# Attention loop of a decoder layer: three local reorderings on ScalarE, TensorE and VectorE

## The chip, the cores and the metric

The kernel runs on one core of a Trainium2 chip. The metric is the device time of one launch in microseconds (us). The core's engines each run their own list of instructions in program order and meet only through semaphores: TensorE (PE in the profile; PEld is its weight load), VectorE (DVE), ScalarE (ACT), GpSimd (POOL) and SyncE (SP), which issues DMAs.

## The reference

One decoder layer on x and ctx of shape 8 x 128 x 128 (batch, tokens, features): a bidirectional state-space block, cross-attention with 16 heads of 8 features, and a mixture of 8 experts with top-1 routing; a layer norm follows each. The change touches the attention:

```python
Q = query @ Wq.T
K = key @ Wk.T
V = value @ Wv.T
scores = jnp.einsum('bqhd,bkhd->bhqk', Qh, Kh) / jnp.sqrt(HEAD_DIM)
attn = jax.nn.softmax(scores, axis=-1)
out = jnp.einsum('bhqk,bkhd->bqhd', attn, Vh)
return out.reshape(b, s, N_HEADS * HEAD_DIM) @ Wo.T
...
x = _layernorm(x + _L0_xattn_ref(x, ctx_1024, ctx_1024, Wq, Wk, Wv, Wo))
x = _layernorm(x + _L0_ffn_ref(x, gate_w, w1, w2))
```

## The kernel before

Everything is float32, written as one explicit list of instructions per engine, so the order on an engine is the order of the Python loops. The state-space block fills the first 239 us or so; then come the projections, the attention loop, the routing of tokens to experts (whose tail overlaps the loop's end), the experts and the last norm.

The attention loop works on 16 items: item n is half of the heads (8 of 16) of batch element n // 2, that is scores of 128 queries x 8 heads x 128 keys, 1024 columns wide. Two items make one batch element b. All engines run the same counter i from 0 to 21, each with its own stage of the pipeline:

- PE at i: `scores(i+1)` (two matmuls of 512 columns, L898); at even i from 6 `turn_out(b)` (one transpose); `turn_probs(i-1)`, eight 128x128 transposes of the exps of item i-1 into banks 4 and 5; `weigh_values(i-2)` (L917, 8 heads); at even i from 6 `project_out(b)` (L939). At odd i from 5 there is `turn_values(b)`, four transposes of the weighted values of a batch element, ahead of `turn_probs`. All transposes have the line L681, that of a helper.
- DVE at i: at odd i from 7 the residual of element i // 2 - 3 (L1269, reads the projection `wo`); `shift_scores(i)`, a maximum over 128 keys (L1208) and a subtraction (L1209), each over 1024 columns; at odd i from 5 `normalize_values` (L1215 and L1218, read what `turn_values` wrote); at even i from 8 the moments for the norm (L1178, L1179).
- ACT at i: the exp of item i (L640); the copy of the transposed exps of item i-1 from banks 4 and 5 to SBUF (L649); at odd i the copies of the weighted values and of the turned output (L486).

Dependences around the change: the exp of item n needs the subtraction of n. `turn_probs(n)` needs the exp of n and also that the copy of item n-1 has emptied banks 4 and 5, since there is one pair of these banks (`pT`). The copy of n needs `turn_probs(n)`. `weigh_values(n)` needs the copy of n. `turn_values(b)`, `turn_out(b)` and `project_out(b)` all write bank 7, in turn; so `turn_values(b)` has to wait until the residual of the element before has read bank 7. `normalize_values(b)` needs `turn_values(b)`, and `turn_out(b)` needs `normalize_values(b)`. The scores have two pairs of banks (0 and 1, 2 and 3), the exps three buffers.

The counter ends the score work at item 15. Behind it the last element's values go through the same stages, and the gate of the experts, the routing and the expert matmuls follow, each needing the one before.

Of the kernel before, what the change touches and what calls it, by code (L numbers as in the profile page):

```python
# [22 lines left out]
def decoder_layer_kernel(nc, x, ctx_1024, in_proj_w, conv_w, conv_bias, x_proj_w, dt_proj_w, dt_proj_bias,  # L23
# [42 lines left out]
    with ExitStack() as ctx:  # L66
# [206 lines left out]
        def was_read(name, last):  # L273
            last.then_inc(read[where[name][0]], 1)
# [209 lines left out]
        def _(sc):  # L484
# [150 lines left out]


            for i in range(LAST):
                if i < 2 * B:
                    wait_read(sc, f"s{i}")
                    sc.activation(prob[i % 3], prob[i % 3], ACT.Exp, scale=SCALE).then_inc(exp_ok, 1)  # L640
                if 1 <= i < 2 * B + 1:
                    c = i - 1
                    to_read(sc, f"pT{c}")
                    if c >= 2:
                        if c % 2:
                            to_read(sc, f"av{c // 2 - 1}")
                        else:
                            sc.wait_ge(av_half, c // 2)
                    was_read(f"pT{c}", sc.activation(probT[c % 2].rearrange("p h k -> p (h k)"),  # L649
                                                     bank[:, 4:6, :].rearrange("p a t -> p (a t)"), ACT.Copy))  # L650
                if i % 2 == 1 and 3 <= i < 2 * B + 3:
                    b = i // 2 - 1
                    if b >= 2:
                        to_read(sc, f"avq{b - 2}")
                    evacuate(f"av{b}", avT[b % 2])
                if i % 2 == 1 and 5 <= i < 2 * B + 5:
                    b = i // 2 - 2
                    if b >= 2:
                        to_read(sc, f"wo{b - 2}")
                    evacuate(f"oT{b}", oT[b % 2], lambda ap: ap[:, 0:S])  # L660
                if i == ROUTE0 + 1:
                    route_exp(0)
# [16 lines left out]
        def _(pe):  # L679
# [296 lines left out]
            for i in range(LAST):  # L976
                if 1 <= i < 2 * B - 1:
                    scores(i + 1)
                if i % 2 == 1 and 5 <= i < 2 * B + 5:
                    turn_values(i // 2 - 2)  # L980
                if i % 2 == 0 and 6 <= i < 2 * B + 6:
                    turn_out(i // 2 - 3)
                if 1 <= i < 2 * B + 1:
                    turn_probs(i - 1)
                if 2 <= i < 2 * B + 2:
                    weigh_values(i - 2)
                if i % 2 == 0 and 6 <= i < 2 * B + 6:
                    project_out(i // 2 - 3)
                if i == ROUTE0:
                    gate_logits(0)  # L990
                if i == ROUTE0 + 2:
                    count_tokens(0)
# [35 lines left out]
        def _(ve):  # L1028
# [167 lines left out]
            evacuate("x1T0", x1T[:, half(0)])  # L1196
            normalize(res1, x1, 0, 1, x1_ok)

            def shift_scores(i):

                c = i % 2
# [3 lines left out]
                    to_read(ve, f"pT{i - 3}")  # L1205
                if i >= 2:
                    wait_read(ve, f"s{i - 2}")
                link(ve.tensor_reduce(rmax[:, c, :], src, AX.X, ALU.max))  # L1208
                was_read(f"s{i}", ve.tensor_tensor(prob[i % 3], src, rmax[:, c, :].unsqueeze(2).to_broadcast([P, CH, S]),  # L1209
                                                   ALU.subtract))  # L1210

# [51 lines left out]
                link(ve.tensor_tensor(p_top, p_top, fits, ALU.mult))  # L1263

            for i in range(LAST + 1):
                if i % 2 == 1 and 7 <= i < 2 * B + 7:
                    b = i // 2 - 3
                    src = to_read(ve, f"wo{b}")
                    was_read(f"wo{b}", ve.tensor_tensor(res2[:, b, :], src[:, 0:D], x1[:, b, :], ALU.add))  # L1269
                if i < 2 * B:  # L1270
                    shift_scores(i)
                if i == 3:
                    evacuate("q1", qT[:, half(1)])
                if i % 2 == 1 and 5 <= i < 2 * B + 5:
# [62 lines left out]
```

## Time and profile before

| | us |
|---|---|
| median of 3 runs | 380.46 (380.46 to 384.38) |
| the profiled execution's own time | 382.21 |
| its span | 380.2 |
| PE busy | 298.9 (79% of the span) |
| DVE busy | 288.6 (76%) |
| ACT busy | 247.2 (65%) |
| attention loop, first to last maximum | 247.58 to 295.76 |

Times in rows are us from the start of the span. An engine's row says when an instruction (or a merged group, "x8" being eight of them) starts and how long it takes, then, in brackets, how long its engine was idle just before it and which instruction released it. An instruction on DVE or ACT starts some 0.1 us ahead of the end of the one before where nothing is waited for, so steps are best read from start to start. Ends of PE's instructions are modelled.

### The profile page before, as it was taken

The numbers are of one execution on the slowest core, as the hardware profiler recorded it, in microseconds if no ns is written. First come the engines' busy times: TensorE is split into PE (matmuls) and PEld (weight loads), VectorE is DVE, ScalarE is ACT, GpSimd is POOL, SyncE is SP. The second block draws the span as 40 slices with busy tenths as digits, with TensorE's granted clock in tenths as the row PEclk, the third lists the DMA queues.
The fourth block names the chain that finished last, engine by engine and source line by source line (L and its number), as shares of the span: only waits on it lengthen the run. The fifth ranks groups of instructions, "written<-read, shape, count | busy, mean of one in ns | idle before, by whom it ended". The sixth has DMA issues, their size and how long they took to land.

```text
span 380.2 us, 5350 instructions
## 1 busy us (share of the span) xinstructions
PE 298.9 (79%) x1677; PEld 182.9 (48%) x1677; DVE 288.6 (76%) x456; ACT 247.2 (65%) x448; POOL 197.4 (52%) x131
## 2 busy tenths in 40 slices
PE   4999704999999998999999999889999753089600
PEld 3444404566565644445455457535565542079600
DVE  2757798899999999999999994799788563102335
ACT  2469777899999998999999984757657510022100
POOL 7400644999999998888988850200000105400073
PEclk9999955999999999999999999999999885559955
DMA  6986030322321333322331000000000000210212
GB/s 160 317 244 221 10 108 1 102 96 81 113 100 66 113 110 110 111 85 86 109 111 55 2 1 2 1 0 2 2 2 0 3 0 28 66 32 17 53 42 69
DMA packets 16767, 26.90 MB, mean 71 GB/s; under 512 B 1964, under 2 KB 10308, under 8 KB 16740
## 3 DMA queue, kind: packets, MB, share of 16 engines
q1 hardware_dynamic: 16036, 25.46, 21.3%
q0 software_dynamic: 704, 1.10, 1.0%
q8 instruction: 14, 0.23, 0.2%
q14 instruction: 13, 0.11, 0.1%
HBM read 24.00 MB, written 2.56 MB: 70 GB/s over the span
## 4 chain that ended last, share of the span: by engine, by line
PE 36%; DVE 30%; issue 11%; POOL 10%; ACT 7%; DMA 4%; SPq 0%; POOLq 0%; DVEq 0%; ACTq 0%
DVE arena L1131 19%; PE bank L681 16%; POOL arena L442 6%; PE bank L1008 3%; DVE acc L1141 3%; PE bank L898 3%; PE bank L917 2%; PE bank L1016 2%; PE bank L817 2%; PE bank L741 2%; PE bank L719 2%; POOL arena L478 2%; ACT arena L649 2%; DMA cw<-in_L_attn_convb_w 1%; DMA arena<-dispatched_tokens 1%
## 5 line engine op out<-in xcount | busy, mean ns | idle before, releaser
L442 POOL TENSOR_TENSOR arena<-arena,k_maskT 128x1024 f32<-128x1024 f32 x64 | 150.9, 2382 | 43.0 <-DVE arena L1118 22.4
L1131 DVE TENSOR_TENSOR_SCAN arena<-bank,arena 128x512 f32<-128x512 f32 x128 | 146.0, 1199 | 0.9 <-ACT bank L574 0.9
L681 PE MATMUL bank<-ident,arena 128*128 128x128 f32 (+1 forms) x726 | 110.4, 289 | 43.0 <-DVE arena L1131 23.5
L681 PEld LDWEIGHTS bank<-ident,arena 128*128 128x128 f32 (+1 forms) x726 | 82.1, 145 | 111.3 <-DVE arena L1131 69.8
L574 ACT ACTIVATE bank<-delta,a_neg 128x508 f32<-128x508 f32 x128 | 88.4, 692 | 10.0 <-DVE arena L1131 6.3
L817 PE MATMUL bank<-conv_in_T,ident 128*128 128x512 f32 x192 | 93.7, 598 | 0.0
L585 ACT ACTIVATE conv_in_T<-bank,c_col 128x256 f32<-128x256 f32 x192 | 80.4, 473 | 11.3 <-PE bank L681 10.6
L454 POOL TENSOR_SCALAR rstd<-moments 128x4 f32<-128x4 f32 x6 | 1.4, 242 | 83.4 <-DVE moments L1179 83.3
L817 PEld LDWEIGHTS bank<-conv_in_T,ident 128*128 128x128 f32 x192 | 31.8, 192 | 15.8 <-issue 14.8
L486 ACT ACTIVATE arena<-bank 128x512 f32<-128x512 f32 (+2 forms) x26 | 12.1, 490 | 32.8 <-PE bank L681 27.4
L1038 DVE COPY arena<-bank 128x160 f32<-128x160 f32 (+2 forms) x20 | 8.1, 433 | 30.9 <-PE bank L1016 17.3
L1141 DVE SCALAR_TENSOR_TENSOR acc<-bank,c_col,acc 128x256 f32<-128x256 f32 x64 | 27.4, 468 | 1.5 <-PE bank L681 1.2
L640 ACT ACTIVATE arena<-arena 128x1024 f32<-128x1024 f32 x16 | 16.9, 1057 | 17.6 <-DVE arena L1209 17.6
L478 POOL DMA_INDIRECT arena<-expert_outputs,take_u x8 | 7.6, 954 | 35.1 <-DMA expert_outputs<-arena 32.9
L1208 DVE TENSOR_REDUCE rmax<-bank 128x8 f32<-128x1024 f32 x16 | 19.4, 1215 | 1.8 <-PE bank L898 1.8
L1209 DVE TENSOR_TENSOR arena<-bank,rmax 128x1024 f32<-128x1024 f32 x16 | 19.6, 1224 | 0.5
L898 PE MATMUL bank<-k_maskT,uT 32*128 32x512 f32 x64 | 18.0, 640 | 0.7 <-DVE arena L1209 0.7
L649 ACT ACTIVATE arena<-bank 128x1024 f32<-128x1024 f32 x16 | 16.2, 1010 | 1.9 <-PE bank L681 1.9
L674 ACT ACTIVATE arena<-bank 128x640 f32<-128x640 f32 x8 | 5.6, 704 | 14.1 <-PE bank L1008 14.1
L719 PE MATMUL bank<-xT,conv_in_T 128*128 128x512 f32 x32 | 14.4, 596 | 0.0
L1008 PE MATMUL bank<-arena,w_sb 128*128 128x160 f32 x64 | 12.1, 345 | 0.6 <-DVE arena L1038 0.6
L1008 PEld LDWEIGHTS bank<-arena,w_sb 128*128 128x128 f32 x64 | 11.0, 226 | 1.0 <-issue 1.0
(155 smaller groups left out, 299.1 us busy)
## 6 DMA issues: line engine op xcount, KB each, us to landing
k_maskT<-b_rows SPq DMA_DIRECT2D x32, 512.0 KB, 3.7
w_sb<-in_L_ffn_w SPq DMA_DIRECT2D x1, 2048.0 KB, 10.6
dispatched_tokens<-zeros SPq DMA_DIRECT2D x1, 640.0 KB, 16.4
expert_outputs<-arena SPq DMA_DIRECT2D x4, 160.0 KB, 2.0
x_tok<-in_x SPq DMA_DIRECT2D x1, 512.0 KB, 3.8
ctx_tok<-in_ctx SPq DMA_DIRECT2D x1, 512.0 KB, 4.1
out<-arena SPq DMA_DIRECT2D x2, 256.0 KB, 2.3
arena<-dispatched_tokens SPq DMA_DIRECT2D x1, 384.0 KB, 3.6
```

Of the source, the lines that this page charges most:

```text
L442: gp.tensor_tensor(dBx[g % 2][h], du[:, dr, h, :], b_bc[:, g % RING, :], ALU.mult).then_inc(dBx_ok, 1)
L574: sc.activation(tiles(bank[:, k % DA_BANKS, :], HB)[:, :, inner], tiles(delta[:, dr, h, half(q)], HB)[:, :, inner], ACT.Exp, scale=a_neg[: ...
L585: sc.activation(y_part[:, p, at:at + DI], hT(g, b), ACT.Copy, scale=c_col[:, dr, b, n:n + 1]).then_inc(part_ok, 1)
L649: was_read(f"pT{c}", sc.activation(probT[c % 2].rearrange("p h k -> p (h k)"), bank[:, 4:6, :].rearrange("p a t -> p (a t)"), ACT.Copy))
L681: return pe.transpose(dst, src, ident[0:src.shape[0], 0:src.shape[0]])
L719: last = pe.matmul(dst, wkT[:, dr, k, :], xT[:, group(th), off:off + S], start=(k == 0), stop=(k == K - 1))
L817: last = pe.matmul(bank[:, Y_BANK + p, :], ident[:, :], y_part[:, p, :], start=(g == 0), stop=False, skip_group_check=True)
L898: last = pe.matmul(bank[:, g, :], qT[in_g, S * b:S * b + S], k_maskT[in_g, b, :, :].rearrange("p j k -> p (j k)"), start=True, stop=True)
L1008: last = pe.matmul(bank[:, where[f"h{e}"][0] + c // 2, at:at + CAP], w1_sb[:, e, P * c:P * c + P], xeT[:, CAP * e:CAP * e + CAP], start=Tr ...
L1131: ve.tensor_tensor_scan(o, a, v, 0.0, ALU.mult, ALU.add).then_inc(scanned, 1)
L1141: ve.scalar_tensor_tensor(acc[:, b, :], hT(g, b), c_col[:, dr, b, n:n + 1], acc[:, b, :], ALU.mult, ALU.add).then_inc(acc_ok, 1)
L1209: was_read(f"s{i}", ve.tensor_tensor(prob[i % 3], src, rmax[:, c, :].unsqueeze(2).to_broadcast([P, CH, S]), ALU.subtract))
```

## The change

Three blocks change places; no instruction is added or removed.

1. ACT: in turn i the copy of the transposed exps of item i-1 stands ahead of the exp of item i.
2. PE: at odd i `turn_values` stands behind `turn_probs`.
3. DVE: at odd i from 7 the residual stands between the maximum and the subtraction of item i, where it stood ahead of the maximum. (The last one, at i = 21, and those of i = 17 and 19, where there is no item any more, stand as before.)

```diff
             for i in range(LAST):
-                if i < 2 * B:
-                    wait_read(sc, f"s{i}")
-                    sc.activation(prob[i % 3], prob[i % 3], ACT.Exp, scale=SCALE).then_inc(exp_ok, 1)
                 if 1 <= i < 2 * B + 1:
                     c = i - 1
                     to_read(sc, f"pT{c}")
...
                     was_read(f"pT{c}", sc.activation(probT[c % 2].rearrange("p h k -> p (h k)"),
                                                      bank[:, 4:6, :].rearrange("p a t -> p (a t)"), ACT.Copy))
+                if i < 2 * B:
+                    wait_read(sc, f"s{i}")
+                    sc.activation(prob[i % 3], prob[i % 3], ACT.Exp, scale=SCALE).then_inc(exp_ok, 1)
...
                     scores(i + 1)
-                if i % 2 == 1 and 5 <= i < 2 * B + 5:
-                    turn_values(i // 2 - 2)
                 if i % 2 == 0 and 6 <= i < 2 * B + 6:
                     turn_out(i // 2 - 3)
                 if 1 <= i < 2 * B + 1:
                     turn_probs(i - 1)
+                if i % 2 == 1 and 5 <= i < 2 * B + 5:
+                    turn_values(i // 2 - 2)
...
+            def add_residual(b):
+                src = to_read(ve, f"wo{b}")
+                was_read(f"wo{b}", ve.tensor_tensor(res2[:, b, :], src[:, 0:D], x1[:, b, :], ALU.add))
...
-                link(ve.tensor_reduce(rmax[:, c, :], src, AX.X, ALU.max))
+                steps[0] += 1
+                ve.tensor_reduce(rmax[:, c, :], src, AX.X, ALU.max).then_inc(dve, 1)
+                max_done = steps[0]
+                if i % 2 == 1 and i >= 7:
+                    add_residual(i // 2 - 3)
+                ve.wait_ge(dve, max_done)
...
             for i in range(LAST + 1):
-                if i % 2 == 1 and 7 <= i < 2 * B + 7:
-                    b = i // 2 - 3
-                    src = to_read(ve, f"wo{b}")
-                    was_read(f"wo{b}", ve.tensor_tensor(res2[:, b, :], src[:, 0:D], x1[:, b, :], ALU.add))
                 if i < 2 * B:
                     shift_scores(i)
+                elif i % 2 == 1 and i < 2 * B + 7:
+                    add_residual(i // 2 - 3)
```

The rows below are the instruction lists themselves, with the semaphores that each waits for. On ACT, at the loop's start (exps of items 0, 1 and 2, copies of items 0 and 1), before the change:

```order
L640 ACTIVATE arena<-arena 128x1024 [waits bank0_read]
L640 ACTIVATE arena<-arena 128x1024 [waits bank2_read]
L649 ACTIVATE arena<-bank 128x1024 [waits bank4_full]
L640 ACTIVATE arena<-arena 128x1024 [waits bank0_read]
L649 ACTIVATE arena<-bank 128x1024 [waits bank4_full]
```

And at the same place with the change, where the exp has the line L650 and the copy L646:

```order
L650 ACTIVATE arena<-arena 128x1024 [waits bank0_read]
L646 ACTIVATE arena<-bank 128x1024 [waits bank4_full]
L650 ACTIVATE arena<-arena 128x1024 [waits bank2_read]
L646 ACTIVATE arena<-bank 128x1024 [waits bank4_full]
L650 ACTIVATE arena<-arena 128x1024 [waits bank0_read]
```

The copy of item i-1, which waits for the transposes (`bank4_full`), now stands ahead of the exp of item i, which waits for the subtraction (`bank0_read` or `bank2_read`).

On PE, at an odd turn in the loop's middle: the scores, the transposes of the values (`bank7_read,bank6_read`), those of the exps (`exp_ok`) and the weighing of the item before.

```order
 L898 MATMUL bank<-k_maskT,uT 128x512 [waits bank7_read,bank2_read,bank0_read]
 L898 MATMUL bank<-k_maskT,uT 128x512
-L681 MATMUL bank<-ident,arena 128x128 [waits bank7_read,bank6_read]
-L681 MATMUL bank<-ident,arena 128x128 x3
-L681 MATMUL bank<-ident,arena 128x128 [waits bank4_read,exp_ok]
-L681 MATMUL bank<-ident,arena 128x128 x7
+L681 MATMUL bank<-ident,arena 128x128 [waits bank4_read,exp_ok]
+L681 MATMUL bank<-ident,arena 128x128 x7
+L681 MATMUL bank<-ident,arena 128x128 [waits bank7_read,bank6_read]
+L681 MATMUL bank<-ident,arena 128x128 x3
 L917 MATMUL bank<-arena,delta 32x128 [waits bank4_read,bank1_read]
 L917 MATMUL bank<-arena,delta 32x128 x7
```

The eight transposes of the exps start by the length of four transposes earlier in PE's list, and those of the values eight later.

On DVE, from the moments of an even turn to the normalization of the odd turn behind it, before the change:

```order
L1178 BN_STATS stats<-arena 128x6 [waits bank7_read]
L1179 BN_AGGR moments<-stats 128x2 [waits dve_steps]
L1269 TENSOR_TENSOR arena<-bank,x_tok 128x128 [waits bank7_full]
L1208 TENSOR_REDUCE rmax<-bank 128x8 [waits bank2_read,bank4_full,bank2_full]
L1209 TENSOR_TENSOR arena<-bank,rmax 128x1024 [waits dve_steps]
L1215 RECIPROCAL inv_sum<-bank 128x16 [waits bank7_full]
```

And with it, where the residual is L1201, the maximum L1213, the subtraction L1218 and the reciprocal L1224:

```order
L1178 BN_STATS stats<-arena 128x6 [waits bank7_read]
L1179 BN_AGGR moments<-stats 128x2 [waits dve_steps]
L1213 TENSOR_REDUCE rmax<-bank 128x8 [waits bank2_read,bank4_full,bank2_full]
L1201 TENSOR_TENSOR arena<-bank,x_tok 128x128 [waits bank7_full]
L1218 TENSOR_TENSOR arena<-bank,rmax 128x1024 [waits dve_steps]
L1224 RECIPROCAL inv_sum<-bank 128x16 [waits bank7_full]
```

The wait for the projection (`bank7_full` of the residual) has moved behind the maximum.

## Rows read from the trace of the kernel before

**Rows 1.** Chain of waits in the loop: start us, length us, engine, tile, line
```profile
254.60 1.06 PE bank L681 x8
...
257.30 1.02 PE bank L681 x8
258.32 0.57 PE bank L917 x16
258.89 1.06 PE bank L898 x4
...
265.70 1.13 PE bank L681 x9
...
275.80 1.46 PE bank L681 x12
277.26 0.62 PE bank L917 x16
...
279.61 1.06 PE bank L681 x8
280.68 0.57 PE bank L917 x16
281.25 0.42 PE bank L939 x2
```

**Rows 2.** Timeline of DVE, a late pair of turns and the last residual of interest
```profile
281.70 0.29 DVE L1269 TENSOR_TENSOR arena<-bank,x_tok 128x128 f32<-128x128 f32 x1 [0.95 <-PE bank L939]
281.91 1.22 DVE L1208 TENSOR_REDUCE rmax<-bank 128x8 f32<-128x1024 f32 x1
283.16 1.22 DVE L1209 TENSOR_TENSOR arena<-bank,rmax 128x1024 f32<-128x1024 f32 x1
284.30 0.25 DVE L1215 RECIPROCAL inv_sum<-bank 128x16 f32<-128x16 f32 x1
...
284.79 1.22 DVE L1208 TENSOR_REDUCE rmax<-bank 128x8 f32<-128x1024 f32 x1
...
288.84 1.22 DVE L1208 TENSOR_REDUCE rmax<-bank 128x8 f32<-128x1024 f32 x1
...
303.88 0.29 DVE L1269 TENSOR_TENSOR arena<-bank,x_tok 128x128 f32<-128x128 f32 x1 [3.74 <-PE bank L939]
```

**Rows 3.** Timeline of ACT: the loop's start, a turn that waits, a late pair, the end
```profile
250.10 1.06 ACT L640 ACTIVATE arena<-arena 128x1024 f32<-128x1024 f32 x1 [2.99 <-DVE arena L1209]
252.49 1.06 ACT L640 ACTIVATE arena<-arena 128x1024 f32<-128x1024 f32 x1 [1.33 <-DVE arena L1209]
...
264.11 1.02 ACT L649 ACTIVATE arena<-bank 128x1024 f32<-128x1024 f32 x1 [0.40 <-PE bank L681]
...
277.50 1.06 ACT L640 ACTIVATE arena<-arena 128x1024 f32<-128x1024 f32 x1 [2.07 <-DVE arena L1209]
278.46 1.01 ACT L649 ACTIVATE arena<-bank 128x1024 f32<-128x1024 f32 x1
279.37 0.76 ACT L486 ACTIVATE arena<-bank 128x512 f32<-128x512 f32 x2
...
298.26 1.06 ACT L640 ACTIVATE arena<-arena 128x1024 f32<-128x1024 f32 x1 [2.07 <-DVE arena L1209]
299.23 1.01 ACT L649 ACTIVATE arena<-bank 128x1024 f32<-128x1024 f32 x1
```

**Rows 4.** Timeline of PE: first and fifth items' transposes, the last item's
```profile
251.21 1.09 PE L681 MATMUL bank<-ident,arena 128*128 128x128 f32 x8
...
262.54 1.53 PE L681 MATMUL bank<-ident,arena 128*128 128x128 f32 x12
...
300.38 1.94 PE L681 MATMUL bank<-ident,arena 128*128 128x128 f32 x8 [1.21 <-ACT arena L649]
```

**Rows 5.** Stretches: length, busy us (x) of PE, PEld, DVE, ACT, POOL; granted clock; DMA
```profile
276.00:283.00 7.00, 6.54 (x66) 4.01 (x65) 5.92 (x10) 4.59 (x6) 0.00 (x0) 1.00 0.00 0
...
301.00:302.00 1.00, 1.00 (x7) 0.92 (x5) 0.00 (x0) 0.00 (x0) 0.00 (x0) 0.50 0.07 16
...
306.00:308.00 2.00, 1.12 (x10) 1.03 (x9) 1.07 (x3) 0.24 (x1) 0.00 (x0) 1.00 0.00 0
```

## Prediction

> **What bounds the kernel now.** I read the stretches first, then the chain of waits in the attention loop, then the timelines of PE, ACT and DVE there. The change touches only this loop, from 247.6 us to some 304 us; before and behind it nothing moves but the start time. In the stretch 276 to 283 PE is busy 6.54 of 7 us, DVE 5.92 and ACT 4.59, at granted clock 1.00 [rows 5], which is 2.4 GHz: PE is the nearest to its limit.
>
> I write T(n) for the start of the eight transposes of the exps of item n, and follow T from item to item.
>
> *Early loop.* From T(1) at 254.60 on, the chain of waits is PE work alone. A turn is transposes 1.02, weighing 0.57, scores 1.06 [rows 1], together 2.65 us. ACT does not bind: the exp of the next item is done well ahead of its transposes, because it stands ahead of the copy.
>
> *Late loop.* A pair of turns lasts 288.84 - 281.91 = 6.93 us [rows 2]. PE's own work in it is 1.46 + 0.57 + 1.06 for the odd turn, 0.11 for the one transpose of the output (nine transposes 1.13 against eight 1.02), and 1.02 + 0.57 + 0.42 + 1.06 for the even turn [rows 1]: 6.27. The rest, 0.66, is one stall: the even turn's transposes (279.61) wait for the copy that empties their banks. That copy starts at 278.46, behind the exp, and the exp starts only at 277.50, when the subtraction is done, ACT having been idle for 2.07 us [rows 3]. So the copy, whose data lie ready since about 277.3 (the twelve transposes of 275.80 end 1.46 later, rows 1 say), waits 1.2 us behind an exp that waits for DVE. The chain runs through the copy (1.01) to PE. DVE too waits in each pair, 0.95 us for the projection ahead of the residual [rows 2]; its work is 6.93 - 0.95 = 5.98 us a pair.
>
> **The change part by part.** No instruction comes or goes; what counts is the new cycle.
>
> *Copy ahead of exp (ACT).* In the late loop this takes the stall's cause away. But it makes a cycle that wasn't there: transposes of item n-1, their copy, the exp of item n (now behind that copy), transposes of item n. Its length c, from rows:
> - transposes to the waiting copy: 264.11 less the start of the eight. They stand behind four others in the twelve that start at 262.54 [rows 3, 4], so at 262.54 + (1.46 - 1.02) = 262.98; 1.13 us. Where PE itself had waited the group is 1.06 and not 1.09 long [rows 1, 4]: 1.10.
> - copy to the next instruction on ACT: 279.37 - 278.46 = 0.91 [rows 3].
> - the exp: 1.06 [rows 3].
> - exp's end to the transposes: 251.16 to 251.21, 0.05 [rows 3, 4]. The nearest other row, a copy's end (279.47) to the transposes at 279.61 [rows 1, 3], gives 0.14, the upper bound. PE was just done with its scores at 251.2 too, so 0.05 hides nothing longer.
>
> So c = 1.10 + 0.91 + 1.06 + 0.05 = 3.12, at most 3.21 with 0.14. **The early loop loses:** 3.12 to 3.21 where it had 2.65, with PE idle 0.5 us a turn. In the late loop c and PE are nearly equal.
>
> *T(n) worked out.* T(0) stays at 251.21 [rows 4]. The copy of item 0 starts at 251.21 + 1.13 = 252.34 (before: behind the exp of 252.49); exp of item 1 at 253.25, ends 254.31; T(1) = 254.36 to 254.45 (before 254.60 [rows 1]). Three cycles: T(4) = 263.72 to 264.08, where it was 262.98. This costs 0.7 to 1.1 us. From T(4) a pair is the larger of PE and cycle in each step: even to odd item PE 1.46 + 0.57 + 1.06 + 0.11 = 3.20 against c = 3.12 to 3.21; odd to even item PE 3.07 against c with 1.13 in place of 1.10, so 3.15 to 3.24. A pair is 6.35 to 6.45. Five pairs: T(14) = 295.5 to 296.3. There are no scores left in the step to item 15, so PE is idle and the step is c: T(15) = 298.6 to 299.5. It was 300.38 [rows 4]. **Gain up to T(15): 0.8 to 1.8; I take the middle, 1.3 us**, since each row bounding c is of this very pair of operations or its neighbour.
>
> *Values behind exps (PE).* Costed in the 3.20 above: with the four transposes in front, the even-to-odd cycle would be 0.44 longer (3.56 to 3.65), so this move is what lets the first one pay, 5 times 0.36 or more. Its price is that the values come 1.02 later, and DVE's normalization with them: filled at T(even) + 1.46 + some 0.1, so DVE normalizes from T + 1.55, is through at T + 2.04 (284.30 to 284.79, 0.49 [rows 2]), and does the next maximum and subtraction (1.25 + 1.22 [rows 2]) by T + 4.5. The exp that needs it may start at T + 3.20 + 1.13 + 0.91 = T + 5.2. Cover: 0.7 us. DVE's own pair is 5.98 or less against 6.4, so it doesn't fall behind.
>
> *Residual between maximum and subtraction (DVE).* The wait for the projection, 0.95 us a pair, now lies behind the maximum. Price on DVE: the residual's step was 0.21 (281.70 to 281.91) and the subtraction waits 1.25 behind the maximum anyway, of which about 0.1 is the gap to an instruction that needn't wait (283.16 to 284.30 is 1.14) [rows 2], so it now costs about 0.1, gain 0.1 a pair on an engine that has 0.4 to spare: nothing in the sum. The value transposes wait for this residual (bank 7); it is done about 1.4 behind the maximum's start, near T(even), and they come at T + 1.02: covered by 1 us. Queued behind the residual's wait are the subtraction and so the odd exp. The projection is ready 2.09 behind the odd T (279.61 to 281.70 [rows 1, 2]), the subtraction is over 1.6 later, at about +3.7, and the odd exp has until about 5.2: cover 1.5 us. No DMA and no queue of SP is passed in any of the moves.
>
> *The end.* At T(15) PE has waited 1.21 us, and the group takes 1.94 instead of 1.02; the stretch 301 to 302 has granted clock 0.50, that is 1.2 GHz [rows 4, 5]. From T(15) to the residual it is 303.88 - 300.38 = 3.50 us [rows 2, 4], where the same work at 2.4 GHz takes 2.09 (above). In the changed kernel PE waits here too, about 1.1 ahead of T(14) and some 0.7 to 0.9 around T(15), with 2.0 us of dense work (twelve transposes and weighing) between. The stretch 306 to 308, with PE busy 1.12 of 2 us, kept clock 1.00 [rows 5]. So I think it likelier than not (about two to one, a judgement and not a row) that T(15) still finds 2.4 GHz: **gain 1.4 us more.** Everything behind (residual, values, gate, routing, experts) hangs on this one step after another and moves as a whole.
>
> The Trainium skill ("TensorE: Matmul & The Clock Gate", section "A second HAM failure mode: psum-queue depth-cycling") speaks against this: in a kernel whose TensorE idles briefly and often between groups, the clock swung between its two levels. The early loop gets just such gaps, 0.5 us in each 3.1. By the rows of this case there is no swing at 0.46 us idle in each pair; by that rule rival 4 would happen, at its price.
>
> **Sum.** 1.3 + 1.4 = 2.7 us. The profiled execution took 382.21 with a span of 380.2; the median of the runs is 380.46. The change is a difference inside the loop, so I take it from the median: 380.46 - 2.7 = **377.8 us**, 0.7% less.
>
> **The rivals.**
> 1. *The order works as above, but the clock at T(15) is 1.2 GHz as before.* Gain 0.8 to 1.8: 379.2 us. For it: PE's idle share around T(14) to T(15) is nearly the old one.
> 2. *Slower, by a longer cycle.* If the exp behind the copy doesn't start 0.1 ahead of the copy's end but 0.05 behind it, and exp to PE is 0.14, then c = 1.13 + 1.01 + 0.05 + 1.06 + 0.14 = 3.39 and T(15) = 254.5 + 14 x 3.39 = 302.0: 1.6 later, 382.1 us. It decides from c = (300.38 - 254.4) / 14 = 3.28 on. Against it: every exp and copy that stand back to back in the rows overlap by 0.1.
> 3. *More gain.* PE alone sets the late loop (6.27), c is 3.1 or less, and the chain behind T(15) loses more gaps (the clock also stays up in the routing): 4 us or more, 376.3. Only the clock speaks for it.
> 4. *The clock falls in the loop*, in the early turns with 0.5 us of idle each. The same PE work at half the clock takes nearly double (1.94 for 1.02): each pair so run costs up to 6 us; one or two give 384 to 390 us. Against it: clock 1.00 with 0.46 idle of 7 and, later, with 0.88 idle of 2 [rows 5].
>
> **How the numbers follow.** About 1% (3.8 us) is what a measurement of this kernel can tell from no change. Forecast 0.50 (own range 376.6 to 378.9), rival 1 0.22, rival 2 0.13, rival 3 0.07, rival 4 0.08. The forecast, rival 1 and rival 2 lie within 1% (382.1 is 0.4%). Faster by over 1%: rival 3 and the very edge of the forecast, 0.09. Slower by over 1%: rival 4, 0.08. Within: 0.83. The range from 376.4 to 381.4 holds the forecast, rival 1, half of rival 2 and a little of rival 3.
>
> **What the profile after would show.** ACT in the early loop alternates copy and exp with PE as the releaser of each copy, T(n) 3.1 to 3.2 apart and PE idle 0.5 ahead of each; T(4) near 263.9. The late pair is near 6.4 us with no stall above 0.15 on PE. The residual has a wait behind the maximum but the exps none for DVE. T(15) near 299, eight transposes in 1.02. I am wrong if an exp in the late loop still names DVE's subtraction as its releaser (then the covers above were too thin), if T(n) are over 3.28 apart, or if a stretch inside the loop has a clock below 1.

## The result, and the profile after

| | before | changed |
|---|---|---|
| median of 15 runs each, us | 381.28 (379.63 to 386.54) | 378.01 (376.98 to 380.23) |
| ratio of the runs | | 0.9897, 95% interval 0.9871 to 0.9923 |
| span of the profiled execution | 380.2 | 376.5 |
| PEclk in the stretch 297 to 304 | 0.76 | 1.00 |

The forecast was 377.8 from 380.46, a ratio of 0.993; the measured one is 0.9897. The range 376.4 to 381.4 holds the time. The ratio leaves out the run of 386.54, over 1.5% above the fastest of its kernel, and is not the quotient of the two medians (0.9914).

The two traces don't start the loop at the same time: the first maximum is at 247.58 before and at 246.41 after, 1.17 us that arose ahead of all that the change touches (over the fourteen traces of this document it lies anywhere from 245.34 to 247.58). So from here on I count from the first maximum, and write T(n), as the prediction does, for the start of the eight transposes of item n's exps.

The early turns first. Chain of waits of the changed kernel (start us, length us, engine, tile, line; L646 is the copy, L650 the exp):

```profile
253.19 1.11 PE bank L681 x8
254.31 0.62 ACT arena L646
254.93 0.30 issue
255.24 1.06 ACT arena L650
256.34 1.11 PE bank L681 x8
```

Where [rows 1] had PE work alone, the chain now runs round the predicted cycle: transposes, copy, exp, transposes, from 253.19 to 256.34, so 3.15 us a turn in place of 2.65. ACT's timeline gives its terms:

```profile
251.16 1.02 ACT L646 ACTIVATE arena<-bank 128x1024 f32<-128x1024 f32 x1 [1.18 <-PE bank L681]
252.08 1.05 ACT L650 ACTIVATE arena<-arena 128x1024 f32<-128x1024 f32 x1
...
276.47 1.02 ACT L646 ACTIVATE arena<-bank 128x1024 f32<-128x1024 f32 x1 [1.18 <-PE bank L681]
277.39 1.05 ACT L650 ACTIVATE arena<-arena 128x1024 f32<-128x1024 f32 x1
278.33 0.80 ACT L486 ACTIVATE arena<-bank 128x512 f32<-128x512 f32 x2
279.67 1.02 ACT L646 ACTIVATE arena<-bank 128x1024 f32<-128x1024 f32 x1 [0.54 <-PE bank L681]
```

Copy to exp is 0.92, the exp 1.05. Behind the loop's very first exp none waits for DVE any more, where [rows 3] had 2.07 us of it in each late pair; every copy waits for PE. PE's timeline, with the start, the late pair and the end:

```profile
250.04 1.09 PE L681 MATMUL bank<-ident,arena 128*128 128x128 f32 x8
...
253.19 1.09 PE L681 MATMUL bank<-ident,arena 128*128 128x128 f32 x8 [0.72 <-ACT arena L650]
...
262.64 1.53 PE L681 MATMUL bank<-ident,arena 128*128 128x128 f32 x12 [0.43 <-ACT arena L650]
...
275.34 1.53 PE L681 MATMUL bank<-ident,arena 128*128 128x128 f32 x12
...
278.43 1.20 PE L681 MATMUL bank<-ident,arena 128*128 128x128 f32 x9
...
281.69 1.53 PE L681 MATMUL bank<-ident,arena 128*128 128x128 f32 x12
...
294.39 1.53 PE L681 MATMUL bank<-ident,arena 128*128 128x128 f32 x12 [1.07 <-ACT arena L650]
...
297.55 1.09 PE L681 MATMUL bank<-ident,arena 128*128 128x128 f32 x8 [0.55 <-ACT arena L650]
```

T(0) to the copy is 251.16 - 250.04 = 1.12; the exp's end at 253.13 to T(1) is 0.06. The late pair is 281.69 - 275.34 = 6.35, with no stall left that the timeline reports. T(4) is at 16.23 from the first maximum (15.40 before), T(14) at 47.98 (48.85), T(15) at 51.14 (52.80). At T(15) the group takes 1.09 and not 1.94: the clock is at 2.4 GHz. DVE in the same pair and at the end:

```profile
280.22 1.23 DVE L1213 TENSOR_REDUCE rmax<-bank 128x8 f32<-128x1024 f32 x1
281.36 0.28 DVE L1201 TENSOR_TENSOR arena<-bank,x_tok 128x128 f32<-128x128 f32 x1
281.56 1.22 DVE L1218 TENSOR_TENSOR arena<-bank,rmax 128x1024 f32<-128x1024 f32 x1
283.25 0.26 DVE L1224 RECIPROCAL inv_sum<-bank 128x16 f32<-128x16 f32 x1 [0.48 <-PE bank L681]
...
299.67 0.29 DVE L1201 TENSOR_TENSOR arena<-bank,x_tok 128x128 f32<-128x128 f32 x1 [1.70 <-PE bank L939]
```

The residual of this pair doesn't wait at all now (0.95 before, [rows 2]), the subtraction starts 1.34 behind the maximum instead of 1.25, and DVE's remaining wait is for the value transposes. The residual of element 5 is the loop's last step that everything behind hangs on: 299.67 - 246.41 = 53.26, where it was 303.88 - 247.58 = 56.30. That is 3.04 us, 1.66 up to T(15) and 1.38 for the clock behind it. Behind this residual the changed kernel's trace is 0.51 us longer (76.83 to the end of the span, against 76.32), so the spans differ by 1.17 + 3.04 - 0.51 = 3.70 us; of these the 1.17 lie ahead of all that was changed.

### The profile page after: what moved, and what is told of

Read it like the earlier page. It is cut to its first block, busy times and chain, and to the rows that moved or that the text cites. A ratio compares the mean times of both kernels' runs of the same rounds, so it can differ in the third digit from the quotient of the medians.

```text
span 376.5 us, 5350 instructions
## 1 busy us (share of the span) xinstructions
PE 296.3 (79%) x1677; PEld 182.3 (48%) x1677; DVE 288.3 (77%) x456; ACT 246.6 (66%) x448; POOL 197.3 (52%) x131
## 4 chain that ended last, share of the span: by engine, by line
PE 38%; DVE 29%; POOL 10%; issue 9%; ACT 8%; DMA 4%; SPq 1%; POOLq 0%; DVEq 0%; ACTq 0%
DVE arena L1131 19%; PE bank L681 17%; POOL arena L442 6%; PE bank L817 3%; PE bank L898 3%; PE bank L1008 3%; DVE acc L1141 3%; PE bank L1016 2%; PE bank L741 2%; PE bank L719 2%; POOL arena L478 2%; PE bank L917 2%; ACT arena L650 2%; ACT arena L646 1%; DMA cw<-in_L_attn_convb_w 1%
## 5 line engine op out<-in xcount | busy, mean ns | idle before, releaser
L681 PE MATMUL bank<-ident,arena 128*128 128x128 f32 (+1 forms) x726 | 109.3, 288 | 41.7 <-DVE arena L1131 23.2
L646 ACT ACTIVATE arena<-bank 128x1024 f32<-128x1024 f32 x16 | 16.4, 1023 | 14.6 <-PE bank L681 14.6
L1213 DVE TENSOR_REDUCE rmax<-bank 128x8 f32<-128x1024 f32 x16 | 19.5, 1219 | 1.9 <-PE bank L898 1.8
L1218 DVE TENSOR_TENSOR arena<-bank,rmax 128x1024 f32<-128x1024 f32 x16 | 19.5, 1222 | 0.4
L650 ACT ACTIVATE arena<-arena 128x1024 f32<-128x1024 f32 x16 | 16.8, 1048 | 3.0 <-DVE arena L1218 3.0
```

The costliest lines, as they stand in the source:

```text
L681: return pe.transpose(dst, src, ident[0:src.shape[0], 0:src.shape[0]])
```

## The experiments

One table first. T(15), the residual of element 5, and the late pair (distance of two late residuals) come from each trace, times from the runs. All ratios are to runs of the kernel before in the same comparison; their medians were 381.28 for the changed kernel, 382.91 for e1 to e4 and 383.37 for e5 and e6, so ratios of different comparisons differ by some tenths of a per cent for this reason alone.

| kernel | late pair | T(15) | residual 5 | median us | ratio (95%) |
|---|---|---|---|---|---|
| before | 6.92 | 52.80 | 56.30 | 381.28 | 1 |
| changed (ACT, PE, DVE) | 6.35 | 51.14 | 53.26 | 378.01 | 0.9897 (0.9871 to 0.9923) |
| e1: ACT | 6.66 | 52.34 | 54.46 | 378.69 | 0.9914 (0.9875 to 0.9954) |
| e2: DVE | 6.27 | 48.94 | 51.04 | 375.1 | 0.9821 (0.9728 to 0.9914) |
| e3: PE | 6.92 | 52.80 | 54.89 | 380.27 | 0.9968 (0.992 to 1.0016) |
| e4: PE, DVE | 6.66 | 51.17 | 53.26 | 377.97 | 0.9893 (0.9796 to 0.9989) |
| e5: ACT, PE | 6.35 | 51.15 | 53.28 | 377.78 | 0.9859 (0.9777 to 0.994) |
| e6: ACT, DVE | 6.66 | 52.34 | 54.46 | 378.5 | 0.9895 (0.9815 to 0.9974) |

My theory was that each step lasts as long as the longest of PE's work, ACT's cycle and DVE's, and that the changed kernel's gain comes from the copy's new place. The rival, which I worked out once the trace showed that the residual waits no more, was that the wait of the residual ahead of the maximum had been the cause all along.

### One part at a time

e1, the ScalarE part alone:

```diff
-                if i < 2 * B:
-                    wait_read(sc, f"s{i}")
-                    sc.activation(prob[i % 3], prob[i % 3], ACT.Exp, scale=SCALE).then_inc(exp_ok, 1)
                 if 1 <= i < 2 * B + 1:
...
                                                      bank[:, 4:6, :].rearrange("p a t -> p (a t)"), ACT.Copy))
+                if i < 2 * B:
+                    wait_read(sc, f"s{i}")
+                    sc.activation(prob[i % 3], prob[i % 3], ACT.Exp, scale=SCALE).then_inc(exp_ok, 1)
```

> Only the ScalarE part of the change (copy ahead of the next exp). Distances are from the start of the first maximum; before / changed kernel: T(4) 15.40 / 16.23, T(15) 52.80 / 51.14, residual of element 5 at 56.30 / 53.26. Theory 'the longest of PE work, ACT cycle and DVE' (ACT cycle now measured as 3.15): early turns 3.15, T(4) 16.2; in the late loop TensorE meets the value transposes ahead of those of the exps, 3.07 + 0.44 = 3.51 in one step, 3.15 in the other, so a pair of 6.66; T(15) near 52.3, residual 5 at 54.4 (full clock) or 55.8 (half clock). Time 0.5 to 1.9 us below before. Rival 'the order on ScalarE by itself does all the work': pair 6.35 and the time of the changed kernel, 3.3 us or more below before.

Measured: pair 6.66, T(15) 52.34, residual 54.46, each within 0.1 us of the theory. The rival falls in the loop. The time did not follow: 378.69 is 4.2 us below the median of 382.91 beside it and not 0.5 to 1.9, because ten of those 19 runs lie in an upper bunch (below) that none of e1's ten shows; below the median of the seven runs in the lower bunch, 380.22, it is 1.5. One late pair of e1, first on ACT, then on PE:

```profile
276.29 1.02 ACT L646 ACTIVATE arena<-bank 128x1024 f32<-128x1024 f32 x1 [1.54 <-PE bank L681]
277.21 1.05 ACT L650 ACTIVATE arena<-arena 128x1024 f32<-128x1024 f32 x1
...
278.31 1.09 PE L681 MATMUL bank<-ident,arena 128*128 128x128 f32 x8 [0.17 <-ACT arena L650]
```

The copy waits only for its transposes, and PE no longer waits for the copy but 0.17 us for the exp behind it. So the copy's new place does take the old stall away, and puts the cycle of 3.15 us in its place.

e2, the VectorE part alone (the kernel before, with the third part of the change's diff):

```diff
-                if i % 2 == 1 and 7 <= i < 2 * B + 7:
-                    b = i // 2 - 3
...
+                if i % 2 == 1 and i >= 7:
+                    add_residual(i // 2 - 3)
...
                 if i < 2 * B:
                     shift_scores(i)
+                elif i % 2 == 1 and i < 2 * B + 7:
+                    add_residual(i // 2 - 3)
```

> Only the VectorE part (residual between maximum and subtraction). Theory 'the wait for the projection sat on the path through subtraction and exp': with it behind the maximum the odd subtraction ends 1.2 us earlier, the exp too, so the copy behind the exp starts when the transposes are done; ScalarE's order needn't change. Then the early turns keep 2.65 (T(4) 15.4), a late pair is TensorE's own 6.27, T(15) near 49.0, residual 5 near 51.1 at full clock: 5 us below before, 2 us below the changed kernel. Rival, from the prediction's account of the stall (the copy's place behind the exp is its cause): the stall stays, pair 6.9, no change within 0.5 us; or a small part of it.

Measured: pair 6.27, T(15) 48.94, residual 51.04. PE's timeline of a late pair:

```profile
272.84 1.53 PE L681 MATMUL bank<-ident,arena 128*128 128x128 f32 x12
...
275.93 1.20 PE L681 MATMUL bank<-ident,arena 128*128 128x128 f32 x9
...
279.11 1.53 PE L681 MATMUL bank<-ident,arena 128*128 128x128 f32 x12
```

No group in this pair, of those left out here either, has idle time ahead of it: the nine transposes of 275.93 (one of the output, eight of exps) run on, where the kernel before had this wait for the copy:

```profile
279.61 1.06 PE L681 MATMUL bank<-ident,arena 128*128 128x128 f32 x8 [0.46 <-ACT arena L649]
```

So with the exp still ahead of the copy, the stall is gone as well. It had two conditions, a copy that stood behind an exp and an exp that waited for a late subtraction, and taking away either is enough: e1 and e5 remove the first, e2 the second. The prediction saw only the first. The early turns keep 2.65 us, since nothing joins copy and exp into a cycle.

e3, the TensorE part alone:

```diff
-                if i % 2 == 1 and 5 <= i < 2 * B + 5:
-                    turn_values(i // 2 - 2)
...
                 if 1 <= i < 2 * B + 1:
                     turn_probs(i - 1)
+                if i % 2 == 1 and 5 <= i < 2 * B + 5:
+                    turn_values(i // 2 - 2)
```

> Only the TensorE part (value transposes behind those of the exps). Theory 'the subtraction sets the odd exp': the even transposes come 0.44 earlier and nobody uses it; pair 6.93, residual 5 at 56.3, no change within 0.4 us. Rival 'every part carries a share': a third of the gain, some 1 us below before.

Measured: pair 6.92 and T(15) 52.80, both unchanged, as the theory had it. The residual of element 5 came at 54.89, 1.41 earlier than expected, since the last eight transposes took 1.07 here, at 2.4 GHz, though the wait ahead of them was the same 1.21 us:

```profile
297.85 0.30 PE L681 MATMUL bank<-ident,arena 128*128 128x128 f32 x1 [0.45 <-DVE arena L1218]
299.37 1.07 PE L681 MATMUL bank<-ident,arena 128*128 128x128 f32 x8 [1.21 <-ACT arena L649]
```

That is a matter of the clock, taken up below.

### Two parts at a time

The edits are the three diffs above in pairs: e4 has those of e2 and e3 (the change without the swap on ScalarE), e5 those of e1 and e3 (without the move on VectorE), e6 those of e1 and e2 (without the move on TensorE).

> The change without its ScalarE part. Theory as for the VectorE part alone: early turns 2.65, pair 6.27, T(15) near 49.3, residual 5 near 51.4 at full clock: about 5 us below before, 1.9 below the changed kernel, the same as the VectorE part alone within 0.4 us. Rival 'the copy must stand ahead of the exp': not better than the changed kernel, pair above 6.35.

Measured: pair 6.66 and not 6.27, residual 53.26 and not 51.4: 2.2 us worse than the VectorE part alone. The expectation failed, and the trace shows why. Timeline of e4 over one pair, all engines (L1218 is the subtraction, L1224 and L1227 the normalization of the values):

```profile
274.30 1.50 PE L681 MATMUL bank<-ident,arena 128*128 128x128 f32 x12 [0.34 <-ACT arena L649]
...
275.83 0.26 DVE L1224 RECIPROCAL inv_sum<-bank 128x16 f32<-128x16 f32 x1 [0.79 <-PE bank L681]
...
276.33 1.21 DVE L1213 TENSOR_REDUCE rmax<-bank 128x8 f32<-128x1024 f32 x1
...
277.58 1.23 DVE L1218 TENSOR_TENSOR arena<-bank,rmax 128x1024 f32<-128x1024 f32 x1
...
278.84 1.06 ACT L640 ACTIVATE arena<-arena 128x1024 f32<-128x1024 f32 x1 [0.78 <-DVE arena L1218]
...
279.80 1.00 ACT L649 ACTIVATE arena<-bank 128x1024 f32<-128x1024 f32 x1
...
280.95 1.50 PE L681 MATMUL bank<-ident,arena 128*128 128x128 f32 x12 [0.34 <-ACT arena L649]
```

Read from top to bottom it is a closed circle: the values, now behind the exps' transposes, are ready 1.53 after T (275.83); the normalization takes 0.50, maximum and subtraction to 278.81; the exp, then the copy behind it (279.80), then the next transposes at 280.95. That is 6.65 us, longer than PE's 6.27. My expectation had counted one pair and not followed the circle into the next. So the TensorE part is worth something only together with the ScalarE part; it costs 2.2 us (53.26 less 51.04) on top of the VectorE part, and nothing alone (e3).

> The change without its VectorE part: copy ahead of exp, values behind exps, residual ahead of the maximum as before. Theory 'once the copy stands ahead of the exp, the ACT cycle (3.15) and TensorE's work (3.17) set the steps, and VectorE has cover': the odd subtraction ends 4.8 behind the odd T two items before, the exp is wanted at 5.2, so nothing is lost; pair 6.35, T(15) 51.1 and residual 5 at 53.3 from the first maximum, as in the changed kernel; time equal to it within 0.4 us. Rival 'the VectorE part carries the gain in the changed kernel as it does alone': pair above 6.6, 1.5 us or more slower than the changed kernel.

Measured: pair 6.35, residual 53.28, against 53.26 of the changed kernel. The residual, ahead of the maximum as before, still waits for the projection, but the exp just ahead of it in time does not wait for DVE (first a row of ACT, then one of DVE):

```profile
281.44 1.05 ACT L650 ACTIVATE arena<-arena 128x1024 f32<-128x1024 f32 x1
281.51 0.29 DVE L1269 TENSOR_TENSOR arena<-bank,x_tok 128x128 f32<-128x128 f32 x1 [0.37 <-PE bank L939]
```

Once the copy stands ahead of the exp, the residual's place is of no matter: the prediction's "nothing in the sum" for it holds.

> The change without its TensorE part: values stay ahead of the exps' transposes. Theory: 3.07 + 0.44 = 3.51 and 3.15, so a pair of 6.66 as with the ScalarE part alone; residual 5 at 54.4 from the first maximum (full clock); 1.2 us slower than the changed kernel. Rival 'with VectorE ahead TensorE's order is of no matter, as with the VectorE part alone': 6.35 or less, residual at 53.3 or earlier.

Measured: pair 6.66, residual 54.46: 1.20 behind the changed kernel, the same as e1. That is what the TensorE part gives where the ScalarE part is in.

e11 takes the ScalarE swap only from turn 5 on, all else as changed:

```diff
+                if i < 5:
+                    wait_read(sc, f"s{i}")
+                    sc.activation(prob[i % 3], prob[i % 3], ACT.Exp, scale=SCALE).then_inc(exp_ok, 1)
                 if 1 <= i < 2 * B + 1:
...
-                if i < 2 * B:
+                if 5 <= i < 2 * B:
```

> The changed kernel, but with the copy ahead of the exp only from turn 5 on; turns 0 to 4 keep the exp first. Theory 'the early loss is the ScalarE cycle and nothing else': T(4) at 15.40 and not 16.23, pair 6.35 from there, residual 5 at 52.4; 0.8 us below the changed kernel. Rival 'the early loss is made good anyway, since TensorE or VectorE bind later': residual at 53.26.

Measured: the copy of item 4 starts at 16.09 and not 17.36, so T(4) is 1.27 us earlier than in the changed kernel (14.96: I had forgotten that the four value transposes no longer stand ahead of it); pair 6.35; residual 51.99, 1.27 less. The early loss is real and is the ScalarE cycle. Its time is 377.25 (376.77 to 378.82, 4 runs), ratio 0.9898 (0.9832 to 0.9964): 0.5 us under the changed kernel beside it (e9 below, 377.74), within what these runs can tell. The traces say where the rest of the 1.27 went: from residual 5 to the end e11 takes 77.69 us and e9 76.71, and the clock falls to 1.2 GHz 57 us behind the first maximum in e11 and 60 us behind it in e9.

### The clock at the end of the loop

The 69 comparison runs of the kernel before lie mostly in two bunches, 379.3 to 380.6 and 382.5 to 386.5, with seven between. Where the clock of each run is known (54 of them, with e1 to e12), the upper bunch has a mean granted clock of 0.891 to 0.894 over the whole span, every other run 0.898 to 0.912. So the bunches go with TensorE's clock. (The profiled execution of the kernel before, 382.21 at 0.904, lies between them.) e7 adds eight transposes to it, read by nobody, in PE's last wait:

```diff
+                if i == 2 * B:
+                    wait_read(pe, "s14")
+                    for h in range(CH):
+                        turn(bank[:, h // 4, S * (h % 4):S * (h % 4) + S], ident[:, :])
                 if 1 <= i < 2 * B + 1:
                     turn_probs(i - 1)
```

> The kernel before with 8 transposes of the unit matrix, whose results nobody reads, put into TensorE's last wait, ahead of the exps' transposes of item 15. Theory 'the clock fell there because TensorE waited': T(15) stays at 52.8 from the first maximum, the group takes 1.02 and not 1.94, residual 5 at 54.9 and not 56.3; time 1.4 us below before. Rival 'the clock there doesn't hang on this wait' (the TensorE part alone also kept 2.4 GHz with the same wait of 1.21): the kernel before itself, run beside it, shows 54.9 too, and there is no difference between the two.

e8 is the kernel before, run beside it.

> The kernel before once more, for its trace: does the fall to 1.2 GHz at T(15) come back? If it belongs to the kernel's own waits: residual 5 at 56.3 again. If it is a matter of where the execution happens to stand: 54.9. The loop itself (T(4) 15.4, pair 6.92, T(15) 52.8) is to repeat within 0.05.

PE's timeline at the end, e7:

```profile
297.96 0.30 PE L681 MATMUL bank<-ident,arena 128*128 128x128 f32 x1 [0.80 <-DVE arena L1222]
298.10 1.04 PE L681 MATMUL bank<-ident 128*128 128x128 f32 x8
299.48 1.06 PE L681 MATMUL bank<-ident,arena 128*128 128x128 f32 x8 [0.34 <-ACT arena L649]
300.47 0.64 PE L917 MATMUL bank<-arena,delta 128*32 128x128 f32 x16
```

and e8:

```profile
299.64 1.06 PE L681 MATMUL bank<-ident,arena 128*128 128x128 f32 x8 [1.21 <-ACT arena L649]
300.63 1.08 PE L917 MATMUL bank<-arena,delta 128*32 128x128 f32 x16
...
302.92 1.09 PE L681 MATMUL bank<-ident,arena 128*128 128x128 f32 x4 [0.47 <-DVE arena L1269]
```

Two stretches of four us, e8 and then e7 (length, busy us of PE, PEld, DVE, ACT, POOL; granted clock; DMA):

```profile
304.00:308.00 4.00, 3.12 (x27) 2.34 (x26) 1.62 (x5) 0.60 (x1) 0.00 (x0) 0.50 0.00 0
...
304.00:308.00 4.00, 2.34 (x15) 2.05 (x16) 2.20 (x10) 0.46 (x2) 0.00 (x0) 0.90 0.00 0
```

T(15) is 52.80 in both, to 0.01. In e8 the fall comes one group later than in the trace of before (the weighing 1.08 instead of 0.64), so neither of my two answers was right as put: the fall came back, at another place, and residual 5 was at 55.65, between 54.89 and 56.30. With the wait filled it did not come there: residual 5 at 54.89, and the granted clock stayed 1.00 up to 307.2. It fell then in e7 too. In fact every one of the fourteen traces has such a fall, at some time from 300.1 to 307.2; what differs is how much work of the chain lies behind it and whether the clock comes back. In the trace of before it was back at 303.5 and cost 1.41 us, all of it ahead of residual 5. In e8 it fell near 300.6 and stayed at 1.2 GHz: 0.76 us up to residual 5, and 2.64 more up to the next residual (7.94 us, against 5.30 in e7). Together with 0.25 behind, that is the 3.65 us by which e8's trace is longer than e7's from the first maximum on.

All ten runs of e7 are from 379.30 to 380.02, with clocks of 0.904 to 0.912, where seven of the ten of e8 are 383.05 and more. The medians are 379.62 and 383.1, the ratios to before 0.9927 (0.9891 to 0.9963) and 0.999 (0.9942 to 1.0039). So filling 1.04 of 1.21 us of one wait, with the loop's schedule untouched, takes away 3.5 us of median. That filling this wait keeps the runs out of the upper bunch is shown. That the wait alone brings on the fall is not: e3's trace has the same wait of 1.21 us without a fall there, and two of e3's ten runs (382.98 and 384.58, clocks 0.894 and 0.892) lie in the upper bunch. What decides in which runs stays open.

This splits the result of the change, roughly. Against the kernel before without the early fall (e7, 379.62) the changed kernel's 378.01 is 1.6 us less, near the 1.66 of T(15); but the two medians are of different comparisons (by the ratios it is 1.1 us), and from the first maximum to the end the changed trace is 1.23 us shorter than e7's: 1.63 at residual 5 and 0.39 behind it won, 0.79 lost behind the experts' first matmul. The rest of the change's gain is that its runs don't show the upper bunch (376.98 to 380.23, clocks 0.906 to 0.911). It shortens PE's idle time ahead of T(15) from 1.21 to 0.55 (297.55 above), but lengthens that ahead of T(14) from 0.48 to 1.07 (294.39 above). That the shorter wait is the reason is argued from e7, not tried on the changed kernel itself.

e12 takes e2 and fills two longer waits behind the loop:

```diff
+            def keep_busy(name, n):
+                dst = to_fill(pe, name)
+                for k in range(n):
+                    turn(dst[:, S * (k % 4):S * (k % 4) + S], ident[:, :])
+
+            keep_busy("x2T1", 12)
             gate_logits(1)
             count_tokens(1)
+            keep_busy("xeT0", 48)
```

> The VectorE part alone plus transposes of the unit matrix, read by nobody, in two waits of TensorE behind the loop: 12 ahead of the second gate (it waits 4.2 us there) and 48 ahead of the tokens' transposes (10.7 us). Theory 'TensorE is at 1.2 GHz behind these waits because it idled': the second gate's two groups take 0.63 and 1.03 (not 1.12 and 1.85), the tokens' transposes and the first expert matmuls 3.7 in all (not 6.65); some 4 us below the VectorE part alone, 371. Rival 'the added transposes end too late, or the clock doesn't rise by them': no gain, or slower by what they overrun.

Measured: 376.1 us (373.9 to 376.94, 4 runs), ratio 0.9839 (0.9773 to 0.9906), no better than the VectorE part alone beside it (e10 below, 375.51 and 0.9841), though one run, 373.9, is below all of that kernel's. In the profiled execution, the longest of the four, the theory failed at both places. PE's timeline of e12:

```profile
307.09 2.77 PE L681 MATMUL bank<-ident 128*128 128x128 f32 x12
311.49 1.12 PE L681 MATMUL bank<-ident,ctx_tok 128*128 128x128 f32 x4 [1.63 <-DVE ctx_tok L1191]
...
316.77 8.26 PE L681 MATMUL bank<-ident 128*128 128x128 f32 x48
327.65 0.66 PE L681 MATMUL bank<-ident,arena 128*128 128x128 f32 x4 [2.62 <-DMA arena<-dispatched_tokens]
328.93 1.13 PE L681 MATMUL bank<-ident,arena 128*128 128x128 f32 x6 [0.62 <-DMA arena<-dispatched_tokens]
330.69 4.60 PE L1015 MATMUL bank<-arena,w_sb 128*128 128x160 f32 x16 [0.63 <-DVE arena L1045]
335.08 1.82 PE L1023 MATMUL bank<-arena,w_sb 128*128 128x160 f32 x8
```

The twelve, 2.77 us at 1.2 GHz, didn't raise the clock (the gate's four transposes still take 1.12). The forty-eight did, near 322.6 us, so the first four of the tokens' transposes took 0.66. But 2.62 us of waiting lay between, and the clock fell again near 329.4, during the six transposes; it was back only near 336, so the experts' first two groups took 4.60 + 1.82. In e2, where the clock was back near 332.7, these took 3.99 and 1.25:

```profile
329.51 3.99 PE L1008 MATMUL bank<-arena,w_sb 128*128 128x160 f32 x16 [0.63 <-DVE arena L1038]
333.34 1.25 PE L1016 MATMUL bank<-arena,w_sb 128*128 128x160 f32 x8
```

What was won at the transposes (0.46 and 0.41, from 1.12 and 1.54 in e2) was lost here (0.61 and 0.57).

### The better version

e9 and e10 are the changed kernel and the VectorE part alone, once more and side by side.

> The changed kernel once more, beside the VectorE part alone and under the same comparison runs: ratio to the kernel before 0.988 to 0.990; residual of element 5 at 53.26 from the first maximum.

> The VectorE part alone once more, next to the changed kernel. Theory (its loop is 2.2 us shorter, 51.04 against 53.26, and nothing behind gives that back): 2 to 3 us less than the changed kernel, 375.3. Rival 'the loop's 2.2 us are lost in the routing, where the clock falls earlier': the two kernels within 1 us.

Measured: e9 377.74 us (377.0 to 379.49, 12 runs), ratio 0.9908 (0.9876 to 0.9939), just above the 0.988 to 0.990 expected, residual 5 at 53.26. e10 375.51 us (374.72 to 375.85, 6 runs), ratio 0.9841 (0.9793 to 0.9888), residual 5 at 51.03. The difference of the medians is 2.2 us, the same as in the loop (53.26 - 51.03), and no run of e10 is as long as the shortest of e9. The third part of the change alone beats all three together. Whether it is more or less than 2% below the kernel before, its interval leaves open.

## Why the prediction was right, and where it was wrong

**The ScalarE cycle.** Forecast 3.12 to 3.21; measured 3.15, made of 1.12, 0.92, 1.05 and 0.06 against 1.10, 0.91, 1.06 and 0.05. Right, and the early loop lost 0.83 us up to T(4) (forecast 0.7 to 1.1).

**The late pair.** Forecast 6.35 to 6.45, measured 6.35. T(14) forecast at 295.5 to 296.3 on the old time axis: measured 47.98 + 247.58 = 295.56. T(15) forecast 298.6 to 299.5, measured 298.72. I took the middle of the range, a gain of 1.3; it was 1.66, since the exp to PE took 0.06 and not 0.14. The value came from the row of this very pair of operations (0.05), and I should have trusted it over the neighbour's.

**The clock.** Forecast 1.4 us at two to one, measured 1.38 between these two traces: T(15) at 2.4 GHz. But as a term of the sum it was misread. I took the clock of one profiled execution as a fixed trait of the kernel before; e3, e7 and e8 show that it falls so early in some executions and not in others, at places that differ, and that this is worth 3.5 us between the medians of e8 and e7. It works on the median by how often it comes, not by 1.4.

**The sum.** 2.7 forecast, 3.04 in the loop of the two traces, 3.3 between the medians, 1.03% by the ratio, right at the edge of what I called the same. That 377.8 met 378.01 is partly luck. The median of three runs from which I subtracted, 380.46, lies in the lower bunch, where all runs of e7 lie too, so there was hardly 1.4 us of clock to win on it; with the 1.66 of T(15) alone it would have given 378.8. The median of 15 runs, 381.28, was 0.8 higher, the gain 0.6 larger, and the two nearly cancel.

**The cause of the stall: half of it.** "In the late loop this takes the stall's cause away" was said of the copy's place. As far as it goes it holds: in the late loop of e1 and e5 no transposes wait for the copy. But e2 shows that the stall goes just as well with ScalarE's order untouched, and without the cycle that cost the early turns 0.83 us. The chain had gone through the copy, and I stopped there; the second condition, an exp idle for 2.07 us until the subtraction was done [rows 3], and behind that DVE's 0.95 for the projection ahead of the maximum [rows 2], were both in the text and not followed. The three parts aren't three shares of one gain: the ScalarE part gives 0.5 up to T(15) alone, the VectorE part 3.9 alone, the two together 0.5, the TensorE part nothing alone, and only with the ScalarE part in does it give 1.2. The gain of the whole change up to T(15) is thus the ScalarE and TensorE parts (e5), and the VectorE part, the best alone, adds nothing to them.

**Values behind exps.** "5 times 0.36 or more", 1.8: measured 1.20 (e6 against changed), pair 6.66 against 6.35. The step mis-sized is that with the values in front: I added the 0.44 to ScalarE's even-to-odd cycle, 3.56. In e6 that step is 3.15, and the 0.44 goes on PE's work in the odd-to-even one, 3.07 + 0.44 = 3.51. The move saves 0.31 in each of four pairs; the fifth odd-to-even step, to item 14, has no scores on PE and gains nothing.

**Residual between maximum and subtraction.** "Now costs about 0.1": 1.34 against 1.25, right. The wait for the projection that was to lie behind the maximum is gone, 0 in each late pair. "Nothing in the sum": right in the changed kernel (e5: 53.28 against 53.26), and far off for the part alone, which the sum didn't ask for.

**The rivals.** The longer cycle (3.28 or more) didn't come: the exp behind the copy starts 0.10 ahead of its end, as every pair in the rows. The clock did not fall inside the loop: every stretch of seven or eight microseconds from 247 to 297 has PEclk 1.00, although PE was idle 0.43 in each early turn. The Trainium skill's warning ("TensorE: Matmul & The Clock Gate", section "A second HAM failure mode: psum-queue depth-cycling", on brief idling between groups) isn't borne out in the loop: 1.00 in all of these stretches. At the loop's end e8 and e7 show that filling a wait of 1.21 us puts the fall off, from 300.6 to 307.2 us.

## What to carry to other kernels

Follow a stall past the instruction that it names: where an in-order engine holds a ready copy behind an exp, ask what the exp waits for, and move that wait first. Every pair of instructions put in a new order on one engine may close a cycle across engines; count it over a whole period, and against the part of the loop that had no stall as well (here the early turns, which lost 0.8 us). Parts of a change should be run alone: the best of the eight combinations here was one part of three.

## What the runs showed of the hardware

TensorE's granted clock fell to 1.2 GHz in every trace between 300.1 and 307.2 us, at the end of the attention loop or behind it, but not at the same work from one execution of the same kernel to the next: at the last item's transposes in one trace of the kernel before (back at 303.5 us), one group later in the other (not back by 320 us), each behind waits of 0.48, 0.80 and 1.21 us. Ten runs of that kernel (e8) were 379.35 to 380.4 or 383.05 to 384.01. Eight transposes of no use in the wait of 1.21 us held all ten runs within 0.72 us of each other. The same remedy in waits of 4.2 and 10.7 us gave nothing: behind the first the clock was at 1.2 GHz as without it. In the second it rose to 2.4 GHz during the 48 transposes, fell again behind 2.62 us of waiting, and was back near 336 us, where it was back near 332.7 in e2.

An instruction without a wait between a maximum and the subtraction that depends on it costs 0.09 us on VectorE (1.34 against 1.25), where it took 0.21 to the next start ahead of the maximum [rows 2].
